# Fourth attention of a four-layer stack: q, k and v projections as three float32r passes, values for pairs of heads, weights split on GpSimd

## The chip, the cores and the metric

The kernel runs on one core of one Trainium2 chip. The metric is the device time of one execution in microseconds (us); less is better. TensorE is PE in the profile, VectorE is DVE, ScalarE is ACT, GpSimd is POOL, and SP issues most of the DMAs.

## What is computed

Four layers in a row, each `x = x + attention(layernorm(x)) * silu(ffn(layernorm(x)))`, on x of 2 x 512 tokens by 256 features, in float32. The change touches the fourth layer. Its attention has 16 heads of 128 features, and its ffn is two ternary linear layers:

```python
def _L3_attn_ref(x, W_K, W_Q, W_V, W_O):
    k = jnp.einsum('ihd,bpd->biph', W_K, x)
    q = jnp.einsum('ihd,bpd->biph', W_Q, x)
    v = jnp.einsum('ihd,bpd->biph', W_V, x)
    scores = jnp.einsum('biph,biqh->biqp', k, q)
    mask = jnp.tril(jnp.ones((pos, pos), dtype=x.dtype))
    masked = scores * mask - jnp.float32(10000000000.0) * (1.0 - mask)
    attn = jax.nn.softmax(masked / jnp.sqrt(jnp.float32(d_head)), axis=-1)
    z = jnp.einsum('biqp,biph->biqh', attn, v)
    z_flat = jnp.transpose(z, (0, 2, 1, 3)).reshape(b, pos, -1)
    out = jnp.einsum('df,bqf->bqd', W_O, z_flat)
    return out
```

## The kernel before

Every engine runs a program of its own, written out in the order in which it is to work, and waits on semaphores. All activations stay in SBUF. `XNT` holds the normalised x with features on partitions (2 chunks of 128) and 1,024 tokens along the free axis; it is made by PE transposes (`ln_transpose`, L706) and ACT copies out of PSUM (`ln_copy`).

The fourth attention is `attention3` in each engine's program. Its unit of work is a step: one tile of 128 queries of one head and one batch b; a head has 8 steps (4 for each batch), with 1, 2, 3, 4 key blocks of 128 (causal). For a step PE computes the scores (`score_tile`, L1024), DVE takes the row maximum (L2104), ACT the exponential (L1555), DVE scales by the inverse sum (L2165, L2167), PE turns the probabilities (`turn_tile`, L1028), ACT copies them to `PT` (L1408), and behind the fourth step of a batch PE multiplies them with v (`value_tiles`, L1033). PE runs step v's turn, then the scores of step v+4, so a step is in flight for four steps.

The projections of the next head lie between these steps by `KV3_STEPS`, all through PSUM bank 7, each waiting until the one before has been copied out (`pj_used`):

```python
KV3_STEPS = {1: ("q", 0), 3: ("k", 0), 4: ("v", 0), 5: ("q", 1), 6: ("k", 1), 7: ("v", 1)}
...
for c in range(DC):
    ins = mm(bank[:, :], wqkv23[:, s, c, :], XNT[:, c, b * SEQ:(b + 1) * SEQ],
             start=c == 0, stop=c == DC - 1)
```

`qk_tile` (L1017) is these two float32 matmuls of 512 columns; `v_tiles` (L1010) is eight of 128 columns (4 token tiles by 2 chunks). A float32 matmul shows as two records in the trace. ACT copies q and v out of PSUM (L1631, L1408), DVE copies k (`store_k`, L2172). SP loads the three weight blocks of the next head (128 KB each) when the last projection with the old ones is done. The six projections of head 0 come first, through banks 6 and 7: those of batch 0, then four score tiles, then the transposes of batch 1, then its projections.

The third ffn (`ffn2`) already uses float32r: matmuls of 512 columns at L1341 and of 256 columns at L1354. In it and behind it lie the layer norm of the fourth layer: DVE statistics, two small POOL operations (`ln_rstd`), DVE scaling (`ln_scale`, L1826). In the last ffn (`ffn3`) DVE first makes ternary weights (`ternarise`) and splits XNT into a rounded and a low part (`xs3`, L2393 and L2394) while PE runs the output projection (L1002).

## Time and profile before

| | |
|---|---|
| median of 3 runs | 1313.78 us (1313.36 to 1317.08) |
| the profiled execution | 1308.78 us, its span 1307.0 us |
| PE busy | 1202.3 us, 92% of the span |
| DVE busy | 720.4 us, 55% |
| ACT busy | 595.7 us, 46% |
| POOL busy | 124.0 us, 9% |
| fourth attention | about 840 to 1201 us of the span |
| last ffn | about 1257 us to the end |

Busy time is the union of an engine's instructions. A timeline row gives an instruction's start and duration; PE's matmuls overlap in the pipeline, so what one run of them takes is read from its start to the start of what follows. What ended an idle time stands in brackets. Windows rows give, in order, the stretch, its length, the busy time of PE, PE's weight loads, DVE, ACT and POOL with the number of instructions, the granted TensorE clock as a share of 2.4 GHz, the DMA share and GB/s.

### The profile page before, as it was taken

How to read it: one execution, taken by the hardware profiler on the slowest of the kernel's cores; microseconds unless marked ns; L12 is line 12 of the kernel's file. 1: busy time of each engine (PE TensorE's matmuls, PEld its weight loads, DVE VectorE, ACT ScalarE, POOL GpSimd, SP SyncE). 2: the span in 40 equal slices, each digit the busy share in tenths (PEclk: the TensorE clock that was granted, in tenths of full speed). 3: DMA queues.
4: the chain of work that ended last, by engine and by line, in shares of the span. 5: the costliest groups of instructions: out<-in, count | busy, mean ns of one | idle time of the engine just before them, and what ended most of it. 6: DMA issues, size and time to landing. Idle time of an engine off the chain costs nothing.

```text
span 1307.0 us, 18353 instructions
## 1 busy us (share of the span) xinstructions
PE 1202.3 (92%) x6204; PEld 764.8 (59%) x6204; DVE 720.4 (55%) x2025; ACT 595.7 (46%) x1502; POOL 124.0 (9%) x145
## 2 busy tenths in 40 slices
PE   5989988888899879999999899999999999998994
PEld 4644444433376454656565588766666666666884
DVE  3778627836242578787888711644444434445537
ACT  2635553787623134545555502544444445444023
POOL 3230023432201200000000100000000000000000
PEclk9979999999999989999999999999999999999997
DMA  8001100320232400000000002100000000000000
GB/s 250 5 17 40 39 28 1 121 60 25 89 94 89 169 13 13 13 13 13 9 9 9 1 1 77 69 25 13 25 13 25 13 25 13 21 17 1 1 1 32
DMA packets 28045, 48.64 MB, mean 37 GB/s; under 512 B 3902, under 2 KB 22302, under 8 KB 26886
## 3 DMA queue, kind: packets, MB, share of 16 engines
q1 hardware_dynamic: 25222, 38.13, 9.0%
q0 software_dynamic: 2736, 9.37, 2.4%
q8 instruction: 52, 0.85, 0.3%
q14 instruction: 35, 0.29, 0.1%
HBM read 40.36 MB, written 9.19 MB: 38 GB/s over the span
## 4 chain that ended last, share of the span: by engine, by line
PE 68%; DVE 13%; issue 9%; ACT 5%; POOL 2%; DMA 1%; SPq 0%; ACTq 0%; POOLq 0%; DVEq 0%
PE bank L1017 13%; PE bank L1033 9%; PE bank L1024 8%; PE bank L1010 5%; PE bank L1002 5%; PE bank L1028 5%; PE bank L1263 2%; PE bank L937 2%; PE bank L926 2%; ACT PT L1527 2%; PE bank L1281 2%; PE bank L847 1%; PE bank L834 1%; PE bank L1354 1%; PE bank L801 1%
## 5 line engine op out<-in xcount | busy, mean ns | idle before, releaser
L1408 ACT COPY R<-bank 128x512 f32<-128x512 f32 (+4 forms) x199 | 106.4, 551 | 314.6 <-PE bank L1033 142.8
L2104 DVE CUSTOM_DVE_ANT_0 bank<-bank,mask_row 128x128 f32<-128x128 f32 (+3 forms) x256 | 127.0, 497 | 173.3 <-PE bank L1024 170.8
L1017 PE MATMUL bank<-XNT,W 128*128 128x512 f32 x416 | 200.2, 605 | 7.4 <-ACT R L1408 3.8
L1555 ACT ACTIVATE R<-bank,nm 128x128 f32<-128x128 f32 (+3 forms) x256 | 136.2, 532 | 110.6 <-DVE nm L2104 109.6
L1024 PE MATMUL bank<-R 128*128 128x512 f32 (+3 forms) x384 | 134.3, 434 | 0.0
L1017 PEld LDWEIGHTS bank<-XNT,W 128*128 128x128 f32 x416 | 75.1, 191 | 100.9 <-issue 92.3
L1002 PE MATMUL bank<-W,R 128*128 128x256 f32 x576 | 125.3, 380 | 3.2 <-ACT R L1408 3.2
L1002 PEld LDWEIGHTS bank<-W,R 128*128 128x128 f32 x576 | 109.1, 190 | 18.7 <-ACT R L1408 2.1
L1028 PE MATMUL bank<-identf,R 128*128 128x128 f32 x640 | 112.3, 275 | 7.1 <-DVE R L2121 5.5
L1033 PE MATMUL bank<-PT,R 128*128 128x128 f32 (+3 forms) x384 | 112.0, 435 | 5.6 <-ACT PT L1408 4.3
L1408 ACT COPY PT<-bank 128x128 f32<-128x128 f32 (+3 forms) x256 | 108.6, 426 | 15.2 <-PE bank L1028 15.1
L1028 PEld LDWEIGHTS bank<-identf,R 128*128 128x128 f32 x640 | 79.2, 141 | 59.2 <-issue 33.7
L1033 PEld LDWEIGHTS bank<-PT,R 128*128 128x128 f32 x384 | 71.2, 190 | 61.4 <-issue 37.8
L1010 PEld LDWEIGHTS bank<-W,XNT 128*128 128x128 f32 x640 | 76.5, 192 | 9.5 <-issue 7.6
L1010 PE MATMUL bank<-W,XNT 128*128 128x128 f32 x640 | 77.9, 275 | 0.0
L1527 ACT ACTIVATE PT<-bank 128x512 f32<-128x512 f32 x128 | 66.5, 608 | 14.1 <-PE bank L926 14.1
L2006 DVE TENSOR_REDUCE W<-bank 128x1 f32<-128x128 f32 (+3 forms) x128 | 57.3, 486 | 18.4 <-PE bank L803 17.4
L1024 PEld LDWEIGHTS bank<-R 128*128 128x128 f32 x384 | 58.2, 191 | 1.1 <-issue 0.5
L1516 ACT ACTIVATE PT<-bank 128x512 f32<-128x512 f32 (+3 forms) x128 | 45.9, 436 | 25.7 <-PE bank L836 25.5
L2121 DVE TENSOR_SCALAR R<-R,erec 128x128 f32<-128x128 f32 (+3 forms) x128 | 51.9, 405 | 5.2
L2167 DVE TENSOR_SCALAR R<-R,erec 128x128 f32<-128x128 f32 (+3 forms) x128 | 49.5, 387 | 5.1
L926 PE MATMUL bank<-R 96*128 96x512 bf16 x128 | 42.1, 392 | 11.0 <-ACT PT L1527 7.3
(285 smaller groups left out, 1800.2 us busy)
## 6 DMA issues: line engine op xcount, KB each, us to landing
W<-in_wq SPq DMA_DIRECT2D x32, 128.0 KB, 2.0
W<-in_wo SPq DMA_DIRECT2D x2, 2048.0 KB, 11.4
W<-in_egu SPq DMA_DIRECT2D x1, 2816.0 KB
W<-in_wk SPq DMA_DIRECT2D x20, 128.0 KB, 2.1
W<-in_wv SPq DMA_DIRECT2D x20, 128.0 KB, 2.0
R<-xg SPq DMA_DIRECT2D x5, 512.0 KB, 4.5
yg<-R SPq DMA_DIRECT2D x5, 512.0 KB, 3.2
W<-in_wa SPq DMA_DIRECT2D x2, 1024.0 KB, 4.8
```

What stands on the lines that cost most here:

```text
L926: mm(PS[n % 3][:, :], kstk[0:KQ, g, b * SEQ + j * P:b * SEQ + (j + 1) * P], qstk[0:KQ, g * GH + h, b * SEQ:(b + 1) * SEQ], start=True, sto ...
L1002: ins = mm(PS[4 + m % 4][:, 0:D], heads[:, k, m * P:(m + 1) * P], w[:, k, :], start=k == 0, stop=k == n - 1)
L1010: ins = mm(bank[:, t * P:(t + 1) * P], XNT[:, c, b * SEQ + t * P:b * SEQ + (t + 1) * P], wqkv23[:, 2, c, :], start=c == 0, stop=c == DC - 1)
L1017: ins = mm(bank[:, :], wqkv23[:, s, c, :], XNT[:, c, b * SEQ:(b + 1) * SEQ], start=c == 0, stop=c == DC - 1)
L1024: return mm(PS[u % 4][:, 0:n], q[:, t * P:n], k[:, 0:n], start=True, stop=True)
L1028: ins = tr(PS[4 + u % 2][:, j * P:(j + 1) * P], Pr[u % 4][:, j * P:(j + 1) * P], identf[:, :])
L1033: ins = mm(PS[6][:, j * P:SEQ], v[:, j, :], PT[:, slot, j, j * P:SEQ], start=j == 0, stop=j == TPB - 1)
L1408: return nc.scalar.copy(dst, src)
L1527: fn(PT[:, s % 2, h, :], PS[n % 3][:, :], ACT.Exp, scale=HD ** -0.5).then_inc(cb["pb_ready"], 1)
L1555: return fn(Pr[c][:, 0:n], PS[c][:, 0:n], ACT.Exp, scale=-1.0, bias=nm[:, c:c + 1], accum_out=esum[:, c:c + 1])
L2006: dve.tensor_reduce(nmx[b][:, t, h:h + 1], PS[banks[i % len(banks)]][:, 0:(t + 1) * P], AX.X, ALU.max, negate=True).then_inc(smax_used, 1)
L2104: return dve.tensor_tensor_reduce(out=s[:, 0:n], in0=s[:, 0:n], in1=mask_row[:, SEQ - n:SEQ], scale=-1.0, scalar=-MASKED, op0=ALU.add, op1 ...
```

## The change

- The rounded copy of XNT (`XH3`, float32r) is now what ACT's `ln_copy` writes, in XNT's place; DVE subtracts it from the same PSUM bank into `XL3` (`low_parts`). The last ffn uses these two and no longer makes `xs3`.
- POOL splits each weight block into a float32r copy and a remainder. The first blocks have parts of their own; all later ones share one pair of buffers for each of q, k and v, so POOL waits until the last projection with the old parts is done.
- q and k: six float32r matmuls of 512 columns for each projection. v: the weights of two heads side by side (256 columns), twelve float32r matmuls of 256 columns for each half of a batch. Head 0 to 13 thus make v for the next pair of heads, two halves each; heads 14 and 15 make none.
- SP's loads go to raw buffers and wait for POOL's parts. `absw` of `ternarise` moves to XN; some semaphores are merged, and DVE's loop in `ffn3` is written out.

```diff
...
-        absw = W2[:, 8192:10240]
+        absw = XN[:, :, :].rearrange("p m d -> p (m d)")
...
+        XH3, XL3 = rounded("x3_high", "XNT", 0, [DC, TOK]), rounded("x3_low", "W2", 8192, [DC, TOK])
...
+        def split_weight(name, inside, first, n):
+            return tuple(rounded(f"{name}_{part}", inside, first + DC * n * k, [DC, n]) for k, part in enumerate(("high", "low")))
+
+        wq3 = [split_weight("wq3_first", "PT", 0, DH), split_weight("wq3", "W2", 4096, DH)]
+        wk3 = [split_weight("wk3_first", "PT", 512, DH), split_weight("wk3", "W2", 4608, DH)]
+        wv3 = [split_weight("wv3_first", "PT", 1024, PAIR), split_weight("wv3", "W2", 5120, PAIR)]
+        raw_q, raw_k = (W1[:, 4096 + 256 * k:4352 + 256 * k].rearrange("p (c n) -> p c n", c=DC) for k in range(2))
+        raw_v = [x.rearrange("p (c n) -> p c n", c=DC) for x in (ptf[:, 2048:2560], W2[:, 6144:6656])]
+        vv3 = [[x[:, 1024 * b:1024 * b + 1024].rearrange("p (t e) -> p t e", t=TPB) for b in range(B)]
+               for x in (R2[:, 2048:4096], XN[:, :, :].rearrange("p m d -> p (m d)"))]
...
         KV3_STEPS = {1: ("q", 0), 3: ("k", 0), 4: ("v", 0), 5: ("q", 1), 6: ("k", 1), 7: ("v", 1)}
...
+        PJ3 = [(kind, b, 0, half) for b in range(B) for kind, half in (("q", 0), ("k", 0), ("v", 0), ("v", 1))]
+        N_FIRST3 = len(PJ3)
+        EVENT3 = {}
+        for head in range(NH - 1):
+            for step, (kind, n) in KV3_STEPS.items():
+                if kind != "v":
+                    EVENT3[head, step] = len(PJ3)
+                    PJ3.append((kind, n, head + 1, 0))
+                elif head // 2 + 1 < NH // 2:
+                    EVENT3[head, step] = len(PJ3)
+                    PJ3.append(("v", head % 2, head // 2 + 1, n))
+
...
             sp.wait_ge(out_ps, NT * 3)
-            sp.dma_start(wqkv23[:, 0], wq[0]).then_inc(ca["wqk"], 16)
-            sp.dma_start(wqkv23[:, 1], wk[0]).then_inc(ca["wqk"], 16)
-            sp.dma_start(wqkv23[:, 2], wv[0]).then_inc(ca["wv"], 16)
+            sp.dma_start(raw_q, wq[0]).then_inc(wq_in, 16)
...
+            sp.dma_start(raw_v[0], wv[0]).then_inc(wv_in, 16)
             sp.dma_start(wo23, W["wo3"]).then_inc(ld["wo23"], 16)
+            sp.wait_ge(ca["w_parts"], split3("q", 0))
+            sp.dma_start(raw_q, wq[1]).then_inc(wq_in, 16)
+            sp.wait_ge(ca["w_parts"], split3("k", 0))
...
             sp.wait_ge(ffn[2]["f"], NT)
...
             sp.dma_start(bout, W["bout3"]).then_inc(ld["ffn3"], 16)
-            with sp.Fori(0, NH - 1) as i:
-                sp.wait_ge(ca["pj_ps"], i * 6 + 5)
-                sp.dma_start(wqkv23[:, 0], wq[i + 1]).then_inc(ca["wqk"], 16)
-                sp.dma_start(wqkv23[:, 1], wk[i + 1]).then_inc(ca["wqk"], 16)
-                sp.wait_ge(ca["pj_ps"], i * 6 + 6)
-                sp.dma_start(wqkv23[:, 2], wv[i + 1]).then_inc(ca["wv"], 16)
+            for i in range(2, NH):
+                sp.wait_ge(ca["w_parts"], split3("q", i - 1))
+                sp.dma_start(raw_q, wq[i]).then_inc(wq_in, 16)
+                sp.wait_ge(ca["w_parts"], split3("k", i - 1))
+                sp.dma_start(raw_k, wk[i]).then_inc(wk_in, 16)
+                if i % 2 == 0 and i // 2 + 1 < NH // 2:
...
+            def split(raw, parts, loaded, earlier, i):
+
+                pool.wait_ge(loaded, 16 * (earlier + i + 1))
+                high, low = parts
+                own(pool.tensor_copy(high[:, :, :], raw))
+                pool.tensor_tensor(low[:, :, :], raw, plain(high[:, :, :]), ALU.subtract).then_inc(ca["w_parts"], 1)
+
+            def split_q(i):
+                if i >= 2:
+                    pool.wait_ge(ca["pj_ps"], PJ3.index(("q", 1, i - 1, 0)) + 1)
+                split(raw_q, wq3[min(i, 1)], wq_in, NH, i)
+
+            def split_k(i):
+                if i >= 2:
+                    pool.wait_ge(ca["pj_ps"], PJ3.index(("k", 1, i - 1, 0)) + 1)
+                split(raw_k, wk3[min(i, 1)], wk_in, KV2, i)
+
+            def split_v(i):
+                if i >= 2:
+                    pool.wait_ge(ca["pj_ps"], PJ3.index(("v", 1, i - 1, 1)) + 1)
+                split(raw_v[min(i, 1)], wv3[min(i, 1)], wv_in, KV2, i)
+
+            pool.wait_ge(corea[0]["o_ps"], NH * B)
+            split_q(0)
+            split_k(0)
+            split_v(0)
             ln_rstd(3)
+            pool.wait_ge(ffn[2]["y_ps"], NT)
+            split_q(1)
+            split_k(1)
+            split_v(1)
+            for i in range(2, NH):
+                split_q(i)
+                split_k(i)
+                if i % 2 == 1 and i // 2 + 1 < NH // 2:
+                    split_v(i // 2 + 1)
...
-                def project(kind, b, n, wn, ahead=0):
-
-                    bank = PS[6 + n % 2] if ahead else PS[7]
-                    pe.wait_ge(ca["wv" if kind == "v" else "wqk"], wn)
-                    if ahead == 0 or n >= 1:
-                        pe.wait_ge(ca["pj_used"], n + 1 - ahead)
-                    ins = v_tiles(bank, b) if kind == "v" else qk_tile(bank, 0 if kind == "q" else 1, b)
+                def project(e):
+
+                    kind, b, i, half = PJ3[e]
+                    first = e < N_FIRST3
+                    bank = PS[6 + e % 2] if first else PS[7]
+                    pe.wait_ge(ca["w_parts"], split3(kind, i))
+                    if not first:
+                        pe.wait_ge(ca["pj_used"], e + 1)
+                    elif e >= 1:
+                        pe.wait_ge(ca["pj_used"], e)
+                    high, low = {"q": wq3, "k": wk3, "v": wv3}[kind][min(i, 1)]
+                    if kind == "v":
+                        for n in range(2):
+                            rows = slice(b * SEQ + (2 * half + n) * P, b * SEQ + (2 * half + n + 1) * P)
+                            for c in range(DC):
+                                for k, (x, w) in enumerate(((XL3, high), (XH3, low), (XH3, high))):
+                                    ins = mm(bank[:, n * PAIR:(n + 1) * PAIR], x[:, c, rows], w[:, c, :],
+                                             start=c == 0 and k == 0, stop=c == DC - 1 and k == 2)
+                    else:
+                        for c in range(DC):
+                            for k, (w, x) in enumerate(((high, XL3), (low, XH3), (high, XH3))):
+                                ins = mm(bank[:, :], w[:, c, :], x[:, c, b * SEQ:(b + 1) * SEQ],
+                                         start=c == 0 and k == 0, stop=c == DC - 1 and k == 2)
                     ins.then_inc(ca["pj_ps"], 1)
...
+                    head = unit // B
+                    e = slice(head % 2 * DH, head % 2 * DH + DH)
+                    value_tiles(b, vv3[head // 2 % 2][b][:, :, e]).then_inc(ca["o_ps"], 1)
...
-                        k += 1
+                    pe.wait_ge(xl_ready, 2 * b + 2)
+                    for e in range(4 * b, 4 * b + 4):
...
-                                         xs3[:, s, c, bass.ds(b * SEQ, SEQ)], start=s == 0 and c == 0, stop=s == 1 and c == DC - 1)
+                                         (XH3, XL3)[s][:, c, bass.ds(b * SEQ, SEQ)], start=s == 0 and c == 0, stop=s == 1 and c == DC - 1)
...
-                    dst = XNT[:, :, 2 * k * P:(2 * k + 2) * P].rearrange("p c (m t) -> p c m t", m=2)
+                    dst = (XH3 if l == 3 else XNT)[:, :, 2 * k * P:(2 * k + 2) * P].rearrange("p c (m t) -> p c m t", m=2)
...
-                            copy(vv[b].rearrange("p j e -> p (j e)"), bank[:, :]).then_inc(ca["pj_used"], 1)
+                            copy(vv3[i % 2][b][:, 2 * half:2 * half + 2, :].rearrange("p t e -> p (t e)"), bank[:, :])\
+                                .then_inc(ca["pj_used"], 1)
...
                         ln_scale(3, 1)
-                    store_k(b, 3 * b + 1, PS[7 - b])
+                        low_parts((2, 3))
+                    store_k(4 * b + 1)
...
+            def low_parts(pairs):
+
+                for k in pairs:
+                    dve.wait_ge(xnt_ready, LN_PAIRS * 3 + k + 1)
+                    src = PS[turn_bank(3, k)][:, :].rearrange("p (m c t) -> p c m t", m=2, c=DC)
+                    high, low = (x[:, :, 2 * k * P:(2 * k + 2) * P].rearrange("p c (m t) -> p c m t", m=2) for x in (XH3, XL3))
+                    tt(low, src, plain(high), ALU.subtract).then_inc(xl_ready, 1)
...
                             hidden(k)
+                        low_parts((0, 1))
...
                 ternarise()
-                own(cp(xs3[:, 0], XNT[:, :, :]))
-                own(tt(xs3[:, 1], XNT[:, :, :], plain(xs3[:, 0]), ALU.subtract))
                 dve.sem_inc(parts_ready, 1)
...
-                with dve.Fori(0, B) as b:
+                for b in range(B):
...
-                        cp(h3s[:, 0, m, :], h3f[m % 4]).then_inc(f["high"], 1)
-                        dve.wait_ge(f["high"], b * 8 + m + 1)
+                        own(cp(h3s[:, 0, m, :], h3f[m % 4]))
...
-    a["wq3"], a["wk3"], a["wv3"] = (heads(g[f"L3_attn_W_{s}"].transpose(0, 2, 1)) for s in "QKV")
+    a["wq3"], a["wk3"] = (heads(g[f"L3_attn_W_{s}"].transpose(0, 2, 1)) for s in "QK")
+    wv = g["L3_attn_W_V"].reshape(NH // 2, 2, DH, DC, P)
+    a["wv3"] = np.ascontiguousarray(wv.transpose(0, 4, 3, 1, 2)).reshape(NH // 2, P, DC, 2 * DH)
```

The order of PE in head 0, the q projection of batch 1 (step 5): a turn of two blocks (L1028), scores of 256 columns (L1024), the projection. Before:

```order
L1028 MATMUL bank<-identf,R 128x128 [waits pt_sb_3,p_ready_3]
L1028 MATMUL bank<-identf,R 128x128
L1024 MATMUL bank<-R 128x256 [waits e_ready_3,pj_used_3]
L1017 MATMUL bank<-XNT,W 128x512 [waits pj_used_3,wqk_3]
L1017 MATMUL bank<-XNT,W 128x512
```

The same place in the changed kernel (L1107 is the turn, L1103 the scores):

```order
L1107 MATMUL bank<-identf,R 128x128 [waits pt_sb_3,p_ready_3]
L1107 MATMUL bank<-identf,R 128x128
L1103 MATMUL bank<-R 128x256 [waits e_ready_3,pj_used_3]
L1216 MATMUL bank<-x_low,wq_high 128x512 [waits pj_used_3,w_parts_3]
L1216 MATMUL bank<-x_high,wq_low 128x512
L1216 MATMUL bank<-x_high,wq_high 128x512
L1216 MATMUL bank<-x_low,wq_high 128x512
L1216 MATMUL bank<-x_high,wq_low 128x512
L1216 MATMUL bank<-x_high,wq_high 128x512
```

Two matmuls became six, at the same place between the steps; the wait for the DMA of the weights became one for POOL's parts.

The order of DVE at the start of the fourth attention, batch 1: the scaling of the layer norm, then the copy of k. Before:

```order
L2104 ISA nm 128x1
L1826 TENSOR_SCALAR XN<-X,mv,rstd 128x256 [waits rstd_ready,var_ready]
L1826 TENSOR_SCALAR XN<-X,mv,rstd 128x256 x3
L2172 COPY R<-bank 128x512 [waits pj_used_3,pj_ps_3]
L2165 RECIPROCAL erec<-esum 128x1 [waits e_ready_3]
```

The same place in the changed kernel:

```order
L2188 ISA nm 128x1
L1910 TENSOR_SCALAR XN<-X,mv,rstd 128x256 [waits rstd_ready,var_ready]
L1910 TENSOR_SCALAR XN<-X,mv,rstd 128x256 x3
L2289 TENSOR_TENSOR x_low<-bank,x_high 128x2x256 [waits xnt_ready] x2
L2258 COPY R<-bank 128x512 [waits pj_used_3,pj_ps_3]
L2249 RECIPROCAL erec<-esum 128x1 [waits e_ready_3]
```

Two subtractions of 512 elements from PSUM now stand between the scaling and the first projection of batch 1.

The order of POOL from the layer norm of the fourth layer on, in the changed kernel (before, the four operations at L528 and L529 were all it had there):

```order
L570 TENSOR_SCALAR rstd<-mv 128x4 [waits var_ready]
L571 TENSOR_TENSOR rstd<-rstd,mhalf 128x4 [waits pool_step]
L728 CAST wq_high<-W 128x256 [waits wq_in,y_ps_2]
L729 TENSOR_TENSOR wq_low<-W,wq_high 128x256 [waits pool_step]
L728 CAST wk_high<-W 128x256 [waits wk_in]
L729 TENSOR_TENSOR wk_low<-W,wk_high 128x256 [waits pool_step]
L728 CAST wv_high<-W 128x512 [waits wv_in]
L729 TENSOR_TENSOR wv_low<-W,wv_high 128x512 [waits pool_step]
L728 CAST wq_high<-W 128x256 [waits wq_in,pj_ps_3]
L729 TENSOR_TENSOR wq_low<-W,wq_high 128x256 [waits pool_step]
```

The splits of the second set come right behind the small operations of the layer norm; those of the third set wait for PE's projections.

## Rows read from the trace of the kernel before

**Rows 1.** The profile's page, part 1: busy time (share of the span) x instructions

```profile
PE 1202.3 (92%) x6204; PEld 764.8 (59%) x6204; DVE 720.4 (55%) x2025; ACT 595.7 (46%) x1502; POOL 124.0 (9%) x145
```

**Rows 2.** Windows, fourth attention and one head: length, busy time per engine, PEclk, DMA share, GB/s

```profile
856.00:1187.00 331.00, 325.50 (x1501) 206.66 (x1500) 139.61 (x515) 162.87 (x451) 0.00 (x0) 1.00 0.06 19
963.35:985.52 22.17, 21.79 (x101) 13.81 (x100) 9.24 (x35) 10.84 (x30) 0.00 (x0) 1.00 0.07 18
```

**Rows 3.** Waits of PE, 863 to 1187: waiting engine, releaser, us in total, times, longest

```profile
PE bank L1017 <- ACT R L1408: 3.8, 14, 0.3
```

**Rows 4.** Timeline of PE, one head: start, us, line, out<-in, records [idle before]

```profile
963.35 1.95 PE L1010 MATMUL bank<-W,XNT 128*128 128x128 f32 x16
965.13 2.32 PE L1033 MATMUL bank<-PT,R 128*128 128x512 f32 x8
...
968.71 1.96 PE L1017 MATMUL bank<-XNT,W 128*128 128x512 f32 x4 [0.27 <-ACT R L1408]
970.50 0.49 PE L1028 MATMUL bank<-identf,R 128*128 128x128 f32 x3
...
972.78 1.88 PE L1017 MATMUL bank<-XNT,W 128*128 128x512 f32 x4
974.49 2.32 PE L1033 MATMUL bank<-PT,R 128*128 128x512 f32 x8
...
979.70 1.96 PE L1017 MATMUL bank<-XNT,W 128*128 128x512 f32 x4
981.49 0.49 PE L1028 MATMUL bank<-identf,R 128*128 128x128 f32 x3
...
982.47 1.92 PE L1017 MATMUL bank<-XNT,W 128*128 128x512 f32 x4
984.22 0.60 PE L1028 MATMUL bank<-identf,R 128*128 128x128 f32 x4
...
985.52 0.49 PE L1010 MATMUL bank<-W,XNT 128*128 128x128 f32 x3
```

**Rows 5.** Timeline of PE, third ffn, one run of float32r matmuls behind transposes

```profile
829.22 1.03 PE L706 MATMUL bank<-identf,XN 128*128 128x128 f32 x8
830.01 0.70 PE L1341 MATMUL bank<-x16r,wa_high 128*128 128x512 f32 x2
830.55 0.63 PE L1341 MATMUL bank<-x16r,wa_low 128*128 128x512 f32 x2
831.02 0.62 PE L1341 MATMUL bank<-x16r,wa_high 128*128 128x512 f32 x2
```

**Rows 6.** Chain of work that ended last, third ffn: 256-column float32r matmuls

```profile
832.10 7.68 PE bank L1354 x64
```

**Rows 7.** Groups of POOL by form: busy us, mean ns | idle before

```profile
L624 POOL TENSOR_TENSOR R<-R,W 128x512 f32<-128x512 f32 x14 | 16.3, 1170 | 39.3 <-ACT R L1673 39.3
...
L565 POOL COPY R<-R 128x512 f32<-128x512 f32 x8 | 4.9, 615 | 79.3 <-DVE R L2025 79.2
```

**Rows 8.** Timeline of POOL in the third attention

```profile
744.62 1.90 POOL L678 CAST x16r<-R 128x2048 fp32r<-128x2048 f16 x1
```

**Rows 9.** Timeline of DVE, before and beside the two POOL casts

```profile
739.98 0.49 DVE L2121 TENSOR_SCALAR R<-R,erec 128x512 f32<-128x512 f32 x1
...
744.87 1.92 DVE L2121 TENSOR_SCALAR R<-R,erec 128x512 f32<-128x512 f32 x1
```

**Rows 10.** Timeline of DVE at the start of the fourth attention

```profile
848.59 1.38 DVE L1826 TENSOR_SCALAR XN<-X,mv,rstd 128x256 f32<-128x256 f32 x4
855.09 0.69 DVE L2172 COPY R<-bank 128x512 f32<-128x512 f32 x1 [5.12 <-PE bank L1017]
```

**Rows 11.** Timeline of PE at the same place

```profile
849.38 1.30 PE L706 MATMUL bank<-identf,XN 128*128 128x128 f32 x8 [1.44 <-DVE XN L1826]
851.35 3.70 PE L1017 MATMUL bank<-XNT,W 128*128 128x512 f32 x8 [0.68 <-ACT XNT L1408]
```

**Rows 12.** Timeline of DVE in the last ffn

```profile
1259.61 0.43 DVE L2401 CAST h_parts<-R 128x512 fp32r<-128x512 f32 x1 [31.67 <-ACT R L1767]
```

More of the change, by code:

```diff
@@ L1635, in store_output, with body @@
                     copy(OT23[:, head, b * SEQ:(b + 1) * SEQ], PS[6][:, :]).then_inc(ca["o_used"], 1)
-                def body(i, first, last):
-                    k = 0 if first else -1
+                def body(i):
+                    first, last = i == 0, i == NH - 1
                     for v in range(TILES):
@@ L1644, in body @@
                             store_output(i if v else i - 1, (v // TPB + 1) % B, i * B + v // TPB - 1)
-                        ev = PLAN3.get(v - 1) if v else PLAN3.get(TILES - 1)
-                        if ev and not (first and v == 0) and not (last and v):
-                            store_projection(ev[0], ev[1], i * npj + 6 + k, PS[7])
-                            k += 1
+                        before = (i, v - 1) if v else (i - 1, TILES - 1)
+                        if before in EVENT3:
+                            store_projection(EVENT3[before])
                         store_pt(i * nt, v, i * B + v // TPB)
-                k = 0
                 for b in range(B):
@@ L1654, in attention3 @@
                         ln_copy(3, (2, 3))
-                    for kind in "qkv":
-                        store_projection(kind, b, k, PS[6 + k % 2])
-                        k += 1
+                    for e in range(4 * b, 4 * b + 4):
+                        store_projection(e)
                     if b == 0:
@@ L1660, in attention3 @@
                             exponent(0, u)
-                body(0, True, False)
-                for i in range(1, NH - 1):
-                    body(i, False, False)
-                body(NH - 1, False, True)
+                for i in range(NH):
+                    body(i)
                 store_output(NH - 1, B - 1, NH * B - 1)
@@ L2180, in body @@
                             maximum(i * nt, v + 4)
-                        if v in PLAN3 and not last:
-                            if PLAN3[v][0] == "k":
-                                store_k(PLAN3[v][1], i * npj + 6 + k, PS[7])
-                            k += 1
+                        if (i, v) in EVENT3:
+                            store_k(EVENT3[i, v])
                 for b in range(B):
```

96 lines of the change are left out of this document (50 added, 46 removed).

## The prediction

> **What bounds the kernel now.** I read the busy times of the page first: PE is busy for 92% of the span, no other engine above 55% [rows 1]. The windows then show what that is in the part that changes: in 331 us of the fourth attention PE is busy for 325.5, at a granted clock of 1.00, which is the 2.4 GHz level; in one head of 22.17 us PE has 21.79, ACT 10.84, DVE 9.24, POOL nothing [rows 2]. The waits of PE there name one releaser, ACT, 14 times 0.3 us [rows 3]. So time that PE's instructions lose in this stage is time that the kernel loses, and the timeline of one head is the view from which the sum is made: what a projection takes is read from its start to the start of the row behind it [rows 4].
>
> **PE, q and k.** The four projections of the head take 1.79, 1.71, 1.79 and 1.75 us, mean 1.76 [rows 4]. The new form is six float32r matmuls of 512 columns. The third ffn has such a run: two matmuls take 0.47 us, and the first two behind transposes 0.54, so 0.07 for the start [rows 5]. Six take 1.41 without a start and 1.48 with one. Of the old four, three have most of such a start in their time (1.79 and 1.75 against 1.71), so I take 1.44. Heads 0 to 15 have 4 each: 64 x (1.76 - 1.44) = **20.5 us** less. Bounds: 64 x 0.28 = 17.9 and 64 x 0.35 = 22.4.
>
> **PE, v.** Eight matmuls of 128 columns take 1.78 us [rows 4]. The new half for two heads is twelve of 256 columns; 64 of them took 7.68 us, 0.12 each [rows 6], so 1.44, with a start 1.51; I take 1.47. The number of projections stays 32 (8 pairs x 2 batches x 2 halves for 16 heads x 2 batches): 32 x (1.78 - 1.47) = **9.9 us** less, bounds 8.6 and 10.9. Together 30.4 us (26.5 to 33.3), and a full head goes from 22.17 to 22.17 - 4 x 0.32 - 2 x 0.31 = 20.3 us. The first round now makes four v halves before the heads' steps and the last two heads make none; the count of 32 has that in it.
>
> The count of passes gives another sum. The Trainium skill, FP8 and Floating Point Precision, § TensorE Precision Notes, says that true FP32 is four passes (the products of the high and low halves of both), so three passes would take three quarters: 1.32 and 1.34 us, 42 us less. The rows say less than that, because a float32r matmul of 512 columns takes 0.235 us against 1.71 / 8 = 0.214 for a quarter of a float32 one [rows 4, 5]; the sum goes by the rows.
>
> **POOL and its cover.** A split is a copy and a subtraction. The nearest rows are 0.615 us for a copy and 1.17 for a two-input operation, both of 512 elements [rows 7]. q and k have 256, so 1.8 us for one split is an upper bound, and a head has at most 1.8 + 1.8 + half of 1.8 (v for every second head) = 4.5 us of POOL in 20.3. What must be in time is the single second set of parts: POOL may overwrite q's only when the projection of batch 1 is done (981.49), and the next head's first one starts at 968.71 + 22.17 = 990.88 [rows 4]. That is 9.4 us, and 8.8 once k and v in between are shorter. 1.8 us, with the load of the next raw block long landed, leaves 7 us. I cost it at 0; without this cover each late microsecond would be one for PE, 15 times over.
>
> **DVE held by POOL.** Beside a POOL cast of 1.90 us [rows 8] a DVE scaling that takes 0.49 us alone took 1.92 [rows 9]. So the two do exclude each other, and the change puts up to 4.5 us of POOL beside DVE in each head. The Trainium skill, SBUF — State Buffer, § Who interferes with whom, calls it an exclusive lock: whichever starts first holds the shared ports for the whole instruction, and a DVE instruction from PSUM with at most one SBUF input is outside it. By that rule the maxima and the copies of k would not be held. DVE's 9.24 us plus all of the 4.5 is 13.7 in a head of 20.3, and the scaled probabilities are ready two steps (some 5 us) ahead of PE's turn. I cost it at 0 between the steps, bounds 0 and 1 us in each of 15 heads, nearer to 0 since PE's waits today are 0.3 us for ACT alone [rows 3].
>
> **The start.** PE stands idle for 1.44 us until the layer norm of batch 1 is scaled and 0.68 for ACT's copy [rows 11]. Two costs land there. The scaling takes 1.38 us from 848.59 [rows 10], and POOL, freed by the small operations at about 845, is splitting q, k and v of the second set until about 850: 0 to 1.2 us (one subtraction in hand), I take 0.7. Behind the ACT copy PE must wait for DVE's second subtraction from PSUM; the nearest row is the copy of k, 0.69 us [rows 10], so **0.7**. The first two subtractions stand in the third ffn, beside the run of 7.68 us on PE [rows 6]; that covers 1.4 us of DVE, which would be the cost without it.
>
> **At nothing.** The split of x removed in the last ffn lay beside the output projection: DVE is idle for 31.67 us behind it [rows 12]. The merged semaphores and DVE's unrolled loop: within 0.5 us either way. SP's loads keep their size and wait for POOL instead of PE.
>
> **Sum.** 30.4 - 0.7 - 0.7 = 29 us less. The profiled execution took 1308.8 us, so 1279.8; the median of the runs shown lies 5.0 us above it, so **1285 us**.
>
> **The rivals.**
>
> *New waits eat half.* The lock delays the scaling of a late tile or the copy of k that the next projection waits for, and PE loses 1 us in each of 15 heads: 15 us of the 29, 1300 us. For it: the fourfold time in rows 9. Against: DVE's spare time. Chance 0.12.
>
> *More than the sum.* A float32r matmul of 512 columns costs a quarter of the float32 one, 0.214 us: six take 1.28, twelve of 256 columns 1.28, so 64 x 0.48 + 32 x 0.50 = 46.7 less, 1268 us. Against: the third ffn runs at 0.235 with nothing in its way [rows 5]. The skill's count of passes, cited above, points the same way. Chance 0.03.
>
> *Slower: the parts come late.* One set of parts for all later heads makes a ring: last projection, POOL's split, first projection of the next head. It decides from 8.8 us for q, and PE is where it was before from 8.8 + 1.9 = 10.7 us, six times the 1.8 of the rows. At 12.5 us (each POOL instruction held by DVE again and again) a head takes 20.3 + 3.7 = 24.0, and 15 heads 15 x 1.8 = 27 us more than before: 1341 us. For it: POOL is one queue, and k and v wait behind q. Against: DVE's longest scaling is 0.49 us, so two instructions can hardly be held for 9 us. Chance 0.03.
>
> *It doesn't do what it says.* If the six matmuls ran as float32 they would take three times 1.76 us. The third ffn shows that the type is honoured. No chance of its own.
>
> **The numbers.** The forecast has 0.82, with 1277 to 1292 as its own range: the bounds of the two PE terms (29 becomes 25 to 32), the start (0 to 2 us), the unrolled loop and some 3 us for how the median falls against a profiled execution. The range to 1299 takes in most of the first rival: 1277 to 1299. A measurement can tell about 0.3%, 4 us, from no change. Faster by more than that: forecast, first and second rival, 0.95 (a little is kept back); within it 0.02; slower 0.03.
>
> **What would show it.** Right: a head lasts 20.3 us; six matmuls on a q or k projection in 1.41 to 1.48 us from start to start and twelve for v in 1.44 to 1.51; PE's waits between the steps still name ACT's copies, 0.3 us each; POOL is busy for 2.5 to 4.5 us in a head; PE's idle time ahead of the projections of batch 1 grows by 0.7 to 2 us; some DVE scalings take over 1 us. Wrong: waits of PE for POOL (parts late), for DVE's scaled probabilities or copies of k (the lock), a granted clock under 1.00 in the attention, or a q projection above 1.6 us.

## The result and the profile after

| | before | after |
|---|---|---|
| median, same chip | 1314.56 us (1313.36 to 1317.08, 4 runs) | 1280.03 us (1278.62 to 1283.87, 4 runs) |
| ratio | | 0.9739 (95% interval 0.9713 to 0.9766) |
| profiled execution, its span | 1308.78, 1307.0 | 1278.62, 1276.8 |
| one head | 22.17 us | 20.13 us |

The changed kernel is faster by 34.5 us of medians, and by 30.2 us of profiled executions. In a second set of runs, on another occasion, the ratio was 0.9759 (0.9726 to 0.9793), 31.3 us of medians (1310.48 to 1279.22).

The busy times of the page, where [rows 1] had 1202.3 for PE and 124.0 for POOL:

```profile
PE 1167.3 (91%) x6200; PEld 775.3 (61%) x6204; DVE 722.9 (57%) x2027; ACT 595.8 (47%) x1502; POOL 174.9 (14%) x225
```

PE has 35 us less, POOL 51 more; DVE and ACT are within 3 us of where they were. The windows, for the steps and for one head, as in [rows 2]:

```profile
859.50:1157.00 297.50, 292.13 (x1483) 215.93 (x1482) 139.93 (x511) 161.78 (x449) 42.81 (x68) 1.00 0.06 17
979.45:999.58 20.13, 19.75 (x102) 14.57 (x101) 9.38 (x34) 10.84 (x32) 4.13 (x6) 1.00 0.08 27
```

PE still fills the head (19.75 of 20.13 us, idle for 0.38 as before), at a granted clock of 1.00. All that POOL does now, 4.13 us in this head with a v split and 2.25 in one without, lies beside it. The waits of PE from 867 to 1157, against [rows 3]:

```profile
PE bank L1216 <- ACT XN L1495: 2.2, 8, 0.3
PE bank L1216 <- ACT R L1495: 1.6, 6, 0.3
```

The same 14 waits of 0.3 us for ACT; none names POOL or DVE. The timeline of PE over the rest of that head and into the next, against [rows 4] (start, us, idle before in brackets):

```profile
992.83 0.47 PE L1216 MATMUL bank<-x_low,wq_high 128*128 128x512 f32 x1
993.14 0.39 PE L1216 MATMUL bank<-x_high,wq_low 128*128 128x512 f32 x1
993.37 0.40 PE L1216 MATMUL bank<-x_high,wq_high 128*128 128x512 f32 x1
...
994.30 0.49 PE L1107 MATMUL bank<-identf,R 128*128 128x128 f32 x3
...
995.24 0.47 PE L1216 MATMUL bank<-x_low,wk_high 128*128 128x512 f32 x1
...
996.70 0.60 PE L1107 MATMUL bank<-identf,R 128*128 128x128 f32 x4
...
1003.00 0.47 PE L1216 MATMUL bank<-x_low,wq_high 128*128 128x512 f32 x1 [0.27 <-ACT R L1495]
...
1004.46 0.49 PE L1107 MATMUL bank<-identf,R 128*128 128x128 f32 x3
```

From start to start, q takes 994.30 - 992.83 = 1.47 and 1004.46 - 1003.00 = 1.46 us, k 996.70 - 995.24 = 1.46. The matmuls behind the first follow at 0.23 to 0.24 us each (993.14, 993.37); their durations of 0.39 overlap and would mislead. The chain of waits gives the tiles as sums (start, us, what, records):

```profile
817.44 7.69 PE bank L1441 x64
...
843.09 3.01 PE bank L1216 x12
846.11 2.87 PE bank L1211 x24
...
855.42 2.98 PE bank L1216 x12
858.40 2.87 PE bank L1211 x24
...
862.26 1.40 PE bank L1216 x6
...
865.94 1.39 PE bank L1216 x6
```

Six matmuls of q or k take 1.39 to 1.40 us here and half of 2.98 or 3.01 at the start; a half of v takes 2.87 / 2 = 1.44. The mean of the head's four q and k tiles is (1.46 + 1.39 + 1.47 + 1.46) / 4 = 1.445 (1.39 from the chain, the rest from the timeline).

**Where the time went, by stage** (marks of PE in the two profiled executions):

| stage | before | after | difference |
|---|---|---|---|
| up to the first projection | 840.29 | 843.09 | +2.8 |
| to the first value matmul | 23.52 | 24.24 | +0.7 |
| to the last value matmul | 334.88 | 301.41 | -33.5 |
| to the end | 108.31 | 108.06 | -0.25 |

The third line is 15 heads x (22.17 - 20.13) = 30.6 and two v halves (2.9) that the first round now makes ahead of the steps, together 33.5. A head's 2.04 us are its six projections. In the chain, where each piece begins at the end of the one before, those of the same head take 1.96, 1.72, 1.96 and 1.76 us for q and k and 1.78 and 1.79 for v before, and 1.62, 1.38, 1.63, 1.43 and 1.43, 1.44 after: 10.97 - 8.93 = 2.04. One q tile and one v tile of it, before and then after:

```profile
979.70 1.96 PE bank L1017 x4
...
977.14 1.79 PE bank L1010 x16
```

```profile
992.83 1.63 PE bank L1216 x6
...
990.63 1.44 PE bank L1211 x12
```

A tile that had to wait is longer in the chain than from start to start (1.96 against 1.79 before, 1.63 against 1.47 after), so only differences are compared between the two readings: a tile of q or k gains 0.335 us by the chain and 0.315 from start to start, one of v 0.35 and 0.34.

The timelines at the start, of PE, DVE and POOL in turn, against [rows 10, 11]:

```profile
852.67 1.30 PE L785 MATMUL bank<-identf,XN 128*128 128x128 f32 x8 [1.53 <-DVE XN L1910]
855.42 0.47 PE L1216 MATMUL bank<-x_low,wq_first_high 128*128 128x512 f32 x1 [1.45 <-ACT x_high L1495]
```

```profile
851.79 1.47 DVE L1910 TENSOR_SCALAR XN<-X,mv,rstd 128x256 f32<-128x256 f32 x4
853.98 1.34 DVE L2289 TENSOR_TENSOR x_low<-bank,x_high 128x512 fp32r<-128x512 f32 x2 [0.72 <-ACT x_high L1495]
```

```profile
850.88 1.27 POOL L729 TENSOR_TENSOR wv_low<-W,wv_high 128x512 fp32r<-128x512 f32 x1
```

The idle time before the transposes grew from 1.44 to 1.53 us, the scaling from 1.38 to 1.47: POOL's last subtraction ended at 852.15 and reached only the scaling's first 0.36 us. The idle time before the projections grew from 0.68 to 1.45. It is put down to ACT, but ACT had been done for 0.8 us: DVE's second subtraction ends at 853.98 + 1.34 = 855.32, and PE starts at 855.42.

### The profile page after: what moved, and what is told of

The parts are those of the page before. It is cut to its first block, busy times and chain, and to the rows that moved or that the text cites. A ratio compares the mean times of both kernels' runs of the same rounds, so it can differ in the third digit from the quotient of the medians.

```text
span 1276.8 us, 18285 instructions
## 1 busy us (share of the span) xinstructions
PE 1167.3 (91%) x6200; PEld 775.3 (61%) x6204; DVE 722.9 (57%) x2027; ACT 595.8 (47%) x1502; POOL 174.9 (14%) x225
## 4 chain that ended last, share of the span: by engine, by line
PE 69%; DVE 14%; issue 9%; ACT 6%; POOL 1%; DMA 1%; SPq 0%; ACTq 0%; POOLq 0%; DVEq 0%
PE bank L1112 9%; PE bank L1103 8%; PE bank L1216 8%; PE bank L1081 5%; PE bank L1107 5%; PE bank L1096 4%; PE bank L1211 4%; PE bank L1350 2%; PE bank L1016 2%; PE bank L1005 2%; PE bank L1401 2%; PE bank L1368 2%; ACT PT L1614 2%; PE bank L926 1%; PE bank L913 1%
## 5 line engine op out<-in xcount | busy, mean ns | idle before, releaser
L1495 ACT COPY R<-bank 128x512 f32<-128x512 f32 (+5 forms) x183 | 97.9, 547 | 292.6 <-PE bank L1112 131.0
L1103 PE MATMUL bank<-R 128*128 128x512 f32 (+3 forms) x384 | 134.3, 434 | 0.0
L1107 PE MATMUL bank<-identf,R 128*128 128x128 f32 x640 | 112.3, 274 | 6.7 <-DVE R L2205 5.5
L1107 PEld LDWEIGHTS bank<-identf,R 128*128 128x128 f32 x640 | 79.1, 141 | 40.8 <-DVE R L2205 20.3
L1112 PE MATMUL bank<-PT,R 128*128 128x512 f32 (+3 forms) x256 | 74.7, 435 | 4.3 <-ACT PT L1495 4.3
L1096 PE MATMUL bank<-XNT,W 128*128 128x512 f32 x160 | 77.3, 608 | 0.7 <-ACT XNT L1495 0.7
L1112 PEld LDWEIGHTS bank<-PT,R 128*128 128x128 f32 x256 | 47.6, 190 | 39.8 <-issue 20.6
L1103 PEld LDWEIGHTS bank<-R 128*128 128x128 f32 x384 | 58.2, 191 | 1.1 <-issue 0.5
L2251 DVE TENSOR_SCALAR R<-R,erec 128x128 f32<-128x128 f32 (+3 forms) x128 | 52.8, 412 | 5.1
L2205 DVE TENSOR_SCALAR R<-R,erec 128x128 f32<-128x128 f32 (+3 forms) x128 | 51.9, 405 | 5.2
L1096 PEld LDWEIGHTS bank<-XNT,W 128*128 128x128 f32 x160 | 30.4, 194 | 38.1 <-issue 31.6
L1642 ACT ACTIVATION_READ_ACCUMULATOR R<-bank,nm 128x1 f32 x256 | 50.4, 197 | 0.0
L1005 PEld LDWEIGHTS bank<-R 96*128 96x128 bf16 x128 | 10.5, 97 | 58.2 <-ACT PT L1614 50.5
```

What stands on the lines that cost most here:

```text
L1005: mm(PS[n % 3][:, :], kstk[0:KQ, g, b * SEQ + j * P:b * SEQ + (j + 1) * P], qstk[0:KQ, g * GH + h, b * SEQ:(b + 1) * SEQ], start=True, sto ...
L1103: return mm(PS[u % 4][:, 0:n], q[:, t * P:n], k[:, 0:n], start=True, stop=True)
L1107: ins = tr(PS[4 + u % 2][:, j * P:(j + 1) * P], Pr[u % 4][:, j * P:(j + 1) * P], identf[:, :])
L1112: ins = mm(PS[6][:, j * P:SEQ], v[:, j, :], PT[:, slot, j, j * P:SEQ], start=j == 0, stop=j == TPB - 1)
L1495: return nc.scalar.copy(dst, src)
L1642: return fn(Pr[c][:, 0:n], PS[c][:, 0:n], ACT.Exp, scale=-1.0, bias=nm[:, c:c + 1], accum_out=esum[:, c:c + 1])
```

## The experiments

All start from the changed kernel unless said otherwise. Ratios are to the kernel before, run on the same chip in the same set.

| run | median (runs) | ratio (95%) | one head |
|---|---|---|---|
| changed, again | 1279.22 (4) | 0.9759 (0.9726 to 0.9793) | 20.13 |
| q and k as float32 | 1302.54 (6) | 0.9931 (0.9908 to 0.9954) | 21.46 |
| v as float32 | 1288.43 (4) | 0.9828 (0.9799 to 0.9856) | 20.74 |
| two passes of three | 1240.06 (4) | 0.9455 (0.9423 to 0.9487) | 17.36 |
| every split twice | 1282.40 (4) | 0.9779 (0.9760 to 0.9797) | 20.15 |
| q parts late, 8 more | 1280.96 (2) | 0.9766 (0.9743 to 0.9789) | 20.15 |
| q parts late, 12 more | 1339.15 (2) | 1.0209 (1.0185 to 1.0234) | 24.34 |
| ACT copies v first | 1273.37 (5) | 0.9704 (0.9685 to 0.9724) | 19.66 |
| v at step 2 | 1276.78 (5) | 0.9739 (0.9716 to 0.9762) | 19.81 |
| both | 1266.09 (5) | 0.9665 (0.9646 to 0.9684) | 19.31 |
| both, low part of x last | 1267.15 (5) | 0.9673 (0.9652 to 0.9694) | 19.31 |

### The changed kernel again

> The changed kernel once more, as the base of the experiments on this chip. Both theories: about 1280 us, 33 to 35 us under the kernel before; a full head lasts 20.13 us as in its first profile.

Its profile repeats the first: span 1276.8, head 20.13, idle times of 1.53 and 1.45 us at the start. It is the base of the next three, which ran in the same set.

### q and k as float32

```diff
-for k, (w, x) in enumerate(((high, XL3), (low, XH3), (high, XH3))):
-    ins = mm(bank[:, :], w[:, c, :], x[:, c, ...], ...)
+ins = mm(bank[:, :], plain(high[:, c, :]), plain(XH3[:, c, ...]), ...)
```

> q and k as two float32 matmuls of 512 columns on the rounded parts (the low parts of x and of the weights are left out of q and k); everything else, POOL's splits too, as in the changed kernel. Theory (PE's time decides, 1.445 us a projection against 1.76): 64 x 0.315 = 20 us more than the changed kernel, about 1300 us, a head of 21.4 us. Rival (the gain came from elsewhere, such as the loads and waits that moved from PE to POOL): under 8 us more.

1302.54 us, 23.3 more than the changed kernel, and a head of 21.46, 1.33 more. So the float32r form of q and k is worth 1.33 / 4 = 0.33 us a tile, with everything else of the change left in place; the 64 tiles are 21.4 us by the chain's 0.335, and with the 1.7 of the clock below that is 23.1 of the 23.3 measured. The loop from first to last values grew by 19.2 us, the stage ahead of it by 3.6. Of these, 1.7 have nothing to do with the type: the first q and k tiles of batch 0 take 3.70 us together, those of batch 1 take 5.37. The windows of batch 1 show why (the granted clock is the third number from the end):

```profile
857.00:859.00 2.00, 1.13 (x2) 0.64 (x3) 0.77 (x2) 0.04 (x1) 0.00 (x0) 0.84 0.00 0
859.00:861.00 2.00, 2.00 (x4) 0.74 (x3) 0.00 (x0) 0.00 (x0) 0.00 (x0) 0.50 0.00 0
861.00:863.00 2.00, 2.00 (x6) 0.85 (x4) 0.00 (x0) 0.60 (x1) 0.00 (x0) 0.81 0.00 0
```

Behind the idle time of 1.45 us the clock is at 0.50, the 1.2 GHz level. In the changed kernel the same stretch reads:

```profile
855.00:857.00 2.00, 1.58 (x7) 1.35 (x8) 0.32 (x1) 0.00 (x0) 0.00 (x0) 1.00 0.00 0
857.00:859.00 2.00, 2.00 (x14) 1.77 (x13) 0.56 (x1) 0.60 (x1) 0.00 (x0) 1.00 0.00 0
```

### v as float32

```diff
-for k, (x, w) in enumerate(((XL3, high), (XH3, low), (XH3, high))):
-    ins = mm(bank[:, n * PAIR:...], x[:, c, rows], w[:, c, :], ...)
+ins = mm(bank[:, n * PAIR:...], plain(XH3[:, c, rows]), plain(high[:, c, :]), ...)
```

> v for pairs of heads as four float32 matmuls of 256 columns for each half on the rounded parts (the low parts are left out of v). Theory: 1.71 to 1.78 us against 1.44, 32 x 0.27 to 0.34 = 9 to 11 us more than the changed kernel, about 1290 us. Rival (the pairing, not the type, gave the gain on v: fewer and wider matmuls): 0 to 3 us more, since the pairing is kept here.

1288.43 us, 9.2 more; a head 20.74, 0.61 more, so 0.3 us for each of its two v tiles. The form of v pays too, and its share is about a third of the whole, as the sum had it. The pairing gives the rest of v's 0.35: as float32 a paired tile takes 1.73 us in the chain, against 1.78 and 1.79 before, so about 0.05. The loop grew by 8.4, the start by 2.7, of which 1.6 are once more the q and k tiles of batch 1 (4.58 us against 3.01 for batch 0), with the clock at 0.50 from 855 to 857.

### Two passes of three

```diff
-(high, XL3), (low, XH3), (high, XH3)
+(low, XH3), (high, XH3)
```

(and the same for v)

> The pass with the low part of x is left out of q, k and v. Theory (PE still decides everything between the steps): a head loses 8 x 0.235 for q and k and 8 x 0.12 for v, 2.84 us, and lasts 17.3 us; in all 64 x 0.47 + 32 x 0.48 = 45 us less than the changed kernel, about 1235 us. Rival (the change has already brought PE close to the chain of scores, maximum, exponential, scaling and turn, or to ACT's copies): new waits eat a third or more, a head of 18.2 us or longer, 30 us less or fewer.

```profile
914.15:931.51 17.36, 16.98 (x86) 12.10 (x85) 9.39 (x35) 10.84 (x31) 2.25 (x4) 1.00 0.07 17
```

The head is 2.77 us shorter for 8 matmuls of 512 columns and 8 of 256 less: 8 x 0.235 + 8 x 0.12 = 2.84. It is bound by PE down to here, with no new wait in the loop: PE is idle for 0.38 us, as before. The median is 39.2 us lower, where 45 were expected. From the first value matmul to the last the kernel takes 39.65 us less; 58 of the 64 q and k tiles and 28 of the 32 v tiles lie there, 40.7 of the 45. The start should have given 4.7 and gave 0.5. The chain shows why:

```profile
855.62 1.78 PE bank L785 x8
...
858.83 3.75 PE bank L1216 x8
862.58 2.06 PE bank L1211 x16
```

PE reaches the layer norm of batch 1 earlier and waits longer for DVE (2.11 us instead of 1.53) and ahead of two halves of v (0.44 for ACT, 0.38 for DVE): 1.4 us. Behind the wait of 2.11 the clock falls: the eight transposes already take 1.78 us instead of 1.32, and it is at 0.50 to 0.57 from 857 to 863. Eight matmuls take 3.75 us, 0.47 each, twice their price. With the transposes (0.46) and the first half of v (0.15) the lower clock costs 2.5 us; waits and clock are 3.9 of the 4.2 that are missing.

### Every split twice

```diff
+for _ in range(2):
     own(pool.tensor_copy(high[:, :, :], raw))
+own(pool.tensor_tensor(low[:, :, :], raw, plain(high[:, :, :]), ALU.subtract))
 pool.tensor_tensor(low[:, :, :], raw, plain(high[:, :, :]), ALU.subtract)
```

> POOL does each copy and each subtraction of a split twice: its busy time in a head with v goes from 4.1 to 8.2 us. Theory (POOL is covered and what it holds up on DVE has slack): within 2 us of the changed kernel. Rival (the lock between POOL and DVE reaches PE): PE's waits grow by up to 1 us in each of 15 heads, 5 to 15 us more.

Two heads of this kernel, and DVE's longest scaling in it:

```profile
880.96:921.26 40.30, 39.53 (x202) 29.15 (x201) 19.71 (x69) 21.64 (x62) 12.75 (x20) 1.00 0.06 20
```

```profile
L2253 DVE TENSOR_SCALAR R<-R,erec 128x512 f32<-128x512 f32 x29 | 19.6, 676 | 1.2
```

POOL works for 12.75 us instead of 6.38, and DVE's scaling of 512 elements takes 676 ns on average instead of 486. A head still takes 20.15 us. One scaling of 512 elements beside POOL, at 904.05, takes 1.41 us. So POOL holds DVE, and between the steps PE doesn't see it. The median is 1.4 us above that of the kernel with 8 more subtractions of the same set. The span is 2.4 us longer than the changed kernel's, and that is at the start: the transposes wait 1.85 + 0.63 us instead of 1.53 (0.95 more), and the first projections of batch 1 take 4.50 us instead of 2.98, at a clock of 0.50 from 857 to 859 (1.52 more).

### q parts late, by 8 and by 12 subtractions

```diff
 own(pool.tensor_copy(high[:, :, :], raw))
+if loaded is wq_in and i >= 2:
+    for _ in range(8):                      # 12 in the second kernel
+        own(pool.tensor_tensor(low[:, :, :], raw, plain(high[:, :, :]), ALU.subtract))
```

> For head 2 and later POOL repeats the subtraction of q's split 8 times more (0.8 us each, 6.4 in all): the parts are ready 7.6 us after PE frees them, the window is 8.7 us. Theory of the ring (the time decides only beyond the window): within 2 us of the changed kernel. Rival (each microsecond of POOL shows in part, by the lock): 3 us or more.

> The same with 12 repeats, 9.6 us: parts after 10.8 us, 2.1 us beyond the window. Theory of the ring: PE waits 2.1 us for POOL in each of 14 heads, 29 us more than the changed kernel, and the change's gain is nearly gone. Rival (more slack than the window shows, or the load of the raw block in the ring as well): under 10 us, or over 45 us more.

With 8, POOL's split of q in one head:

```profile
956.40 0.40 POOL L728 CAST wq_high<-W 128x256 fp32r<-128x256 f32 x1 [9.15 <-PE bank L1219]
956.87 6.39 POOL L731 TENSOR_TENSOR wq_low<-W,wq_high 128x256 fp32r<-128x256 f32 x8
963.34 0.73 POOL L732 TENSOR_TENSOR wq_low<-W,wq_high 128x256 fp32r<-128x256 f32 x1
```

From 956.40 to 964.07 are 7.7 us, and nothing changes: head 20.15, median 1280.96. With 12, first POOL's last subtraction, then PE, then PE's waits from 900 to 1100:

```profile
997.50 0.40 POOL L728 CAST wq_high<-W 128x256 fp32r<-128x256 f32 x1 [12.24 <-PE bank L1219]
...
1007.73 0.72 POOL L732 TENSOR_TENSOR wq_low<-W,wq_high 128x256 fp32r<-128x256 f32 x1
```

```profile
1008.51 0.50 PE L1219 MATMUL bank<-x_low,wq_high 128*128 128x512 f32 x1 [2.80 <-POOL wq_low L732]
...
1009.52 0.63 PE L1219 MATMUL bank<-x_low,wq_high 128*128 128x512 f32 x1
1009.95 0.63 PE L1219 MATMUL bank<-x_high,wq_low 128*128 128x512 f32 x1
```

```profile
PE bank L1219 <- POOL wq_low L732: 22.4, 8, 2.8
```

The split lasts 10.95 us and PE waits 2.8 in every head. The window is thus between 7.7 and 10.95 us; in the changed kernel it can be read as 1003.00 - 994.30 = 8.7, and POOL's start (0.23 behind PE) and PE's (0.06 behind POOL) are in it. Here PE's q projection ends at 997.27 and the next begins at 1008.51, 11.24 us later, which is 2.5 beyond the window. A head grew by 24.34 - 20.13 = 4.2 us. The other 1.7 are the clock behind the wait:

```profile
1005.00:1009.00 4.00, 1.20 (x7) 0.75 (x6) 1.83 (x8) 2.19 (x8) 3.61 (x7) 1.00 0.01 2
1009.00:1011.00 2.00, 2.00 (x7) 1.46 (x6) 0.00 (x0) 0.00 (x0) 1.92 (x3) 0.52 0.35 99
1011.00:1013.00 2.00, 2.00 (x10) 1.40 (x9) 0.19 (x1) 1.08 (x2) 0.52 (x1) 0.63 0.34 76
```

The matmuls at 1009.52 and 1009.95 are 0.43 us apart instead of 0.235. PE is busy throughout the last two windows, at 0.52 and 0.63 of the clock, so 2 x 0.48 + 2 x 0.37 = 1.7 us of its full speed are missing. The expectation had the wait nearly right (2.1 us for 2.5) and the time wrong: 58 us more than the kernel with 8 more subtractions, where 29 were expected. In 14 heads the clock is 24 us of the difference, and the longer wait 6. This kernel is 2.1% slower than the one before the change (ratio 1.0185 to 1.0234). So the slower rival is a real mechanism, and the changed kernel, whose split of q ends at 995.73 and is needed by 1003.00, is 7.2 us of POOL away from it.

POOL's twelve subtractions are one row from 997.97 to 1007.65. Beside it DVE's maxima of 384 and 512 elements take 0.57 and 0.68 us and its copy of k 0.69, as without POOL; its scalings of 256, 384 and 512 take 0.61, 0.98 and 0.76 instead of 0.35, 0.42 and 0.49.

### Two waits for ACT, and both together

The 0.27 us before each head's first q projection is a wait until ACT has copied v out of bank 7; ahead of that copy ACT stores the output of the batch. The first kernel swaps the two, the second moves a v projection to an earlier step.

```diff
-if v % TPB == 0 and not (first and v == 0):
-    store_output(...)
 before = ...
 if before in EVENT3:
     store_projection(EVENT3[before])
+if v % TPB == 0 and not (first and v == 0):
+    store_output(...)
```

```diff
-KV3_STEPS = {1: ("q", 0), 3: ("k", 0), 4: ("v", 0), ...}
+KV3_STEPS = {1: ("q", 0), 2: ("v", 0), 3: ("k", 0), ...}
```

> ACT copies the v projection of step 7 out of PSUM before it copies the output of the values that PE is then still computing, no longer behind it. Theory (the q projection of step 1 waits for that copy; the row in front of it names 0.27 us, and from the end of the scores to its start there is 0.44): 0.3 to 0.44 us in each of 14 or 15 heads, 4 to 6 us less than the changed kernel. Rival (the copy of the output, now later, delays ACT's next turns): no gain.

> The first v half of a head is projected at step 2, no longer at step 4 (which the change allows, since v has two buffers). Theory (the q projection of step 5 starts 0.28 us late, for ACT's copy of that v): 0.28 us in each of 14 heads, about 4 us less than the changed kernel. Rival (steps 1, 2 and 3 now each carry a projection through the one bank, and the wait moves there): no gain, or 1 to 3 us more.

> The last two edits together: if both waits are real and apart, 8 to 10 us less than the changed kernel, a head of 19.4 us, about 1271 us. Rival (one wait behind the other): no more than the better of the two alone.

The swap gives 0.47 us a head and a ratio of 0.9704. From the first projection to the last value matmul its profile is 6.7 us shorter, where 4 to 6 were expected. The move alone gives 0.32 a head in the profile and 4.0 us over the same stretch, as expected; its ratio, 0.9739 (0.9716 to 0.9762), can't be told from the changed kernel's 0.9759 or 0.9739. Together they give 0.82 a head and 11.0 us over the stretch, about the sum of the two, so the waits are apart (8 to 10 were expected). Moving a half of v into the stage ahead of the first values costs 0.5 us of it there. The ratio is 0.9665 (0.9646 to 0.9684), whose interval lies below both of the changed kernel's:

```profile
880.60:899.91 19.31, 19.31 (x101) 14.70 (x101) 9.14 (x34) 11.00 (x32) 2.25 (x4) 1.00 0.05 15
```

In this head PE is busy for all of the 19.31 us. At 1266.09 us this is faster than both kernels.

A wait shown as 0.27 us gives 0.47, because the row in front of it covers a part of the wait: matmuls overlap, and their ends in the profile are modelled. From the turn in front of the q projection to the turn behind it PE takes 984.33 - 981.78 = 2.55 us in the changed kernel and 884.88 - 882.84 = 2.04 with the swap. The whole gain lies at this place, 0.27 of it shown as idle time and the rest inside the rows beside it. The wait that the move takes away is shown as 0.11 of idle time, and is 0.28 from start to start (992.83 - 992.12 = 0.71, where two scores of 256 columns take 0.43).

### Both, and the passes with the low part of x last

```diff
-pe.wait_ge(xl_ready, 2 * b + 2)
 for e in range(4 * b, 4 * b + 4):
     project(e)
...
-for c in range(DC):
-    for k, (w, x) in enumerate(((high, XL3), (low, XH3), (high, XH3))):
+for k, (w, x) in enumerate(((low, XH3), (high, XH3), (high, XL3))):
+    if first and kind == "q" and k == 2:
+        pe.wait_ge(xl_ready, 2 * b + 2)
+    for c in range(DC):
+        ...
```

> Both edits, and in every q and k projection the two matmuls with the low part of x come last, so that at the start PE waits for DVE's subtraction only there. Theory: PE's 1.45 us of idle time ahead of the projections of batch 1 shrinks by 0.7 us; 0.7 us less than the two edits alone, too little for the times to tell, so the timeline decides. Rival: the wait is only moved, since the subtraction ends after the first four matmuls (0.94 us).

```profile
853.38 0.74 PE L1218 MATMUL bank<-x_high,wq_first_low 128*128 128x512 f32 x2 [0.68 <-ACT x_high L1496]
```

The idle time is back at 0.68 us, as in [rows 11], so the added 0.77 was indeed the wait for DVE's second subtraction. It was not moved to the last matmuls: the twelve of q and k take 3.06 us instead of 3.00, and from the first projection to the first values PE takes 0.7 us less than without this edit. That can't be told by the runs: 0.9673 against 0.9665.

## Why the prediction was right

The forecast was 1285 us (1277 to 1299), the median is 1280.03. The sum stood against the profiled execution: 29 less was forecast, 30.2 were measured. The other 3.6 us are the median's distance from the profiled execution, taken as 5.0, and 1.4 in the changed kernel's runs.

That 29 stands so close to 30.2 is in part luck. From the first projection on, the changed kernel is 0.7 - 33.5 - 0.25 = -33.0 us, 4.0 more than the sum had; 2.8 us were lost ahead of it, in code that the change doesn't touch (see below, not foreseen). Of the 4.0, 2.1 are the heads (15 x (2.04 - 1.90)), 0.5 the start, which cost 0.9 and not 1.4, and 0.4 the projections ahead of the first values, which gave more than those of a head (below). Of the last 1.0, 0.25 lie behind the last value matmul, and the rest is not assigned.

**What bounds the kernel.** Held. PE fills the head before and after, and two experiments that only change PE's matmuls (q and k as float32, two passes of three) move the head by PE's own price, 1.33 and 2.77 us. PE's idle time in them stays at 0.38 us a head.

**q and k.** 1.44 forecast, 1.445 measured: 64 x (1.76 - 1.445) = 20.2 us against 20.5. The start of 0.07 us is to be seen: tiles with it take 1.46, the others 1.39. By the chain it is 0.335 a tile, 21.4 us.

**v.** 1.47 forecast, 1.44 measured: 32 x (1.78 - 1.44) = 10.9 against 9.9. It is twelve times the 0.12 of [rows 6], without the 0.07 for a start of which half had been put in. Both tiles together give 31.1, at 30.4 forecast, and by the chain's 0.335 and 0.35 it is 32.6. All of a head's gain is in its tiles; nothing outside them gave any.

**The count of passes.** Three quarters of the old time would be 42 us less, the rows had 30.4, and the tiles measured 31.1. The Trainium skill, FP8 and Floating Point Precision, § TensorE Precision Notes, gives true FP32 as four passes. Taken as a ratio of times, the trace doesn't agree with it: a tile of three passes takes 1.445 us of 1.76, which is 0.82 and not 0.75. The second rival (0.214 us for a float32r matmul) fell with it: they follow at 0.23 to 0.24.

**POOL's cover.** Held, and with more room than the sum gave it. A split of q takes 0.40 + 0.73 us with its gap 1.2, not 1.8. A head has 4.13 us of POOL with a v split and 2.25 without one, so the lower end of the 2.5 to 4.5 forecast was too high. The window of 8.8 us is 8.7.

**DVE held by POOL.** The cost of 0 between the steps held, also with POOL doing twice the work, so the first rival (15 us) fell. That some scalings would take over 1 us was wrong for this kernel (with every split done twice one took 1.41). The scalings of 256 elements, after and before:

```profile
L2251 DVE TENSOR_SCALAR R<-R,erec 128x256 f32<-128x256 f32 x29 | 13.5, 466 | 1.1
```

```profile
L2167 DVE TENSOR_SCALAR R<-R,erec 128x256 f32<-128x256 f32 x29 | 10.3, 354 | 1.1
```

That is 0.11 us on average, and 3 us of DVE over the loop. POOL's instructions are short (0.4 to 1.3 us), the splits start at fixed places of a head, and the scalings that they meet are few. The maxima and the copies of k kept their times (429 and 692 ns for 256 and 512 elements in both kernels), also beside the twelve subtractions in a row. The Trainium skill, SBUF — State Buffer, § Who interferes with whom, says that a DVE instruction with at most one SBUF input, outside the 2-port perf modes, does not contend with GpSimd. The trace agrees: the maxima and the copies of k, which read PSUM and at most one tile of SBUF, are not held.

**The start.** 0.7 for the held scaling was 0.09: POOL's last subtraction overlapped only the scaling's first 0.36 us. 0.7 for DVE's second subtraction was 0.77. The stage as a whole grew by 0.7 us: two v halves more (+2.9), cheaper tiles (-3.0 for six of q and k and two of v) and these costs (+0.9). The six of q and k give 2.3 and not six times 0.315: the chain has two at 3.70 us twice, one at 1.98 and one at 1.72 before, and 3.01, 2.98, 1.40 and 1.39 after.

**Slower, the parts late.** The place was right and the point of decision too (8.8 us, tried at 7.7 and 10.95), but the price of one late microsecond was taken as one. It was 4.2 us for 2.5 of lateness, because the clock fell behind the wait. The price of lateness was mis-sized: the kernel with 12 more subtractions lands at 1339 with a split of 10.95 us, where the rival needed 12.5 us for 1341.

**Not foreseen.** The first projection comes 2.8 us later in the profiled execution, in code that the change doesn't touch; the run of 64 matmuls in the third ffn takes 7.69 us as before but starts at 817.44 instead of 814.64. In the profiles of all eleven other runs here it starts between 816.08 and 820.43, so it is the one profiled execution of the kernel before, itself 5 us under its median, that is early. In the three later sets of runs the kernel before has medians of 1310.17 to 1311.81 us, 1.4 to 3.0 above that execution; the 5.0 us that the forecast added came from three runs that lay above all three. The two traces come apart at about 330 us, in the second attention, where PE waits for ACT 0.65 and 1.48 us at two places at which it waited 0.26 before. What sets these was not tried, and stays open.

## What to carry to other kernels

Price a tile from start to start, in the same kernel, for the very shape and type that the new code will use; two such rows gave the two large terms here within 1.3 us each. Where a helper engine has one buffer for a ring, compute the window and the point from which it decides, and price lateness there above one to one, since a wait that lets the clock fall costs again behind it. Once the large term is taken, look at the short waits that recur in every unit: an order of two copies on ACT and one step of a table, 0.82 us a head, gave 11 us more. Read such a wait from start to start, since the idle time that the profile shows is only a part of it.
